# Hyperbolic attention of an adaLN-attention-FFN layer: projections and attention loop in one program, with loop steps between the last projections

## The chip, the cores and the metric

The kernel runs on one core of a Trainium2 chip. The metric is the device time of one execution in microseconds (us), the median of several runs. The engines of the core run beside each other and are ordered by semaphores alone: PE (matmuls), DVE (VectorE), ACT (ScalarE), POOL (GpSimd) and SP, which issues most of the DMAs.

## What is computed

The reference is one transformer layer on `x` of 32 x 64 x 256 in float32. Its stages are a mixture of eight experts and a shared one, a hyperbolic causal attention with a residual, three dense or routed feed-forward parts, a rotary attention and a last mixture of experts. The change lies in the hyperbolic attention:

```python
importance = sigmoid(x @ w_sur + b_sur)
spikes = importance > threshold
q, k, v = split(x @ W_qkv + b_qkv)           # 16 heads of 16
# for q and k, per head, with u0 the first element and u1.. the other fifteen:
nomin = sqrt(max(-u0**2 + sum(u1..**2), 1e-8))
time, space = cosh(nomin), sinh(nomin) * u1.. / nomin
neg_inner = tq @ tk.T - sq @ sk.T
scores = -arccosh(max(neg_inner, 1 + 1e-7))**2 / sqrt(16)     # causal
y = (softmax(scores) * spikes) @ v
x = x_residual + y @ W_out + b_out
```

## The kernel before

All of the stage's data stays in SBUF. There are 2048 tokens, in `NP = 16` blocks of 128 tokens and in `TT = 4` pieces of 512 (`TW`). Matrix products with W_qkv are made in three passes, because source and weights are split in a rounded part (`hi`) and a rest (`lo`).

`hyper_attention` has two programs, one after the other.

The first is the projection program. ACT rounds a piece of 512 tokens (`round_src`, L1703), DVE takes the rest (`split_src`, L1765). For each block i, PE makes q and k as one 512-column product in six matmuls, then v as 256 columns in six matmuls and one for the bias (L1682, L1688); both have two PSUM banks. DVE adds the bias and so takes q and k out of PSUM (L1852), ACT squares them (L1737) and takes v (L1742), and DVE sums the squares of each head (`space_norm`, L1784). v is copied by DMA to the places of both halves (L1663) and blocked out by head on ACT (`block_values`, L1711). The norms are a chain of 15 small DVE operations for half of the blocks at once (`norms`, L1796 to L1831), each waiting for the one before (`link`), and five exponentials on ACT (L1719 to L1725). Group 0 (blocks 0 to 7) runs between blocks 9 to 14, group 1 (blocks 8 to 15) behind the last block. The spike logits are 256 narrow matmuls of PE behind the last projection (L1694), then an exponential on ACT and three DVE operations (L1774 to L1778).

Then all engines meet at a barrier, and `hyper_units` begins. It is a software pipeline over 16 units of 128 query rows. Its loop has 25 steps; in step u each engine does the phases of the list `order`, phase with lag l for unit u - l. For one unit the path is: `stretch` on DVE scales q and k (L1538, lag 1), `turn` on PE transposes them (L1416, L1420, lag 1), `take_q` on ACT (L1493, 1), `block_k` on DVE (L1546, 2), `score` on PE (L1434, 3), `clamp` on DVE (L1553, 3), square, logarithm and root on ACT (L1498, L1502, L1506; 3, 4, 4), `root_add` on POOL (L1588, 4), logarithm and square on ACT (L1511, L1515; 4, 5), `mask` on POOL (L1593, 5), `top` on DVE (L1558, 6), `shift` on POOL (L1598, 5), `exponential` on ACT (L1522, 6), `p_turn` on PE and `p_take` on ACT (L1443, L1527; 7), `mix` on PE and `scale_y` on DVE (L1454, L1567; 8), and the output projection and the residual add (L1464 to L1576; 8, 9). Even units have 512 scores per row, odd ones 1024. Each engine executes its phases in the written order, so a phase that waits holds all that stand behind it on its engine.

Of the kernel before, what the change touches and what calls it, by code (L numbers as in the profile page):

```python
# [1250 lines left out]
class AttentionWeights:  # L1251


    def __init__(self, nc, m, ctx, raw, tag, w_qkv, w_out, b_qkv=None, b_out=None, w_sur=None, side=None):
# [7 lines left out]
        if b_qkv is not None:  # L1262
            self.bias, self.bo, self.ws = sb("bias", [P, 2 * D]), sb("bo", [P, KC]), sb("ws", [P, KC])
            self.vb = sb("vb", [P, D])
            self.loads += [(self.bo[:], col(b_out)), (self.ws[:], col(w_sur)),
                           (self.vb[:], b_qkv[2 * D:].unsqueeze(0).to_broadcast([P, D]))]
# [4 lines left out]
            self.vb_hi, self.vb_lo, self.vb_both, self.share = row("vb_hi", D), row("vb_lo", D), row("vb_both", D), row("share", P)  # L1271
        part = lambda name: sb(name, [P, KC, 3 * D], F32R)
        self.wq_hi, self.wq_lo = part("wq_hi"), part("wq_lo")

        self.wq = raw.enter_context(nc.sbuf_tensor(f"{tag}_wq", [P, KC, 3 * D], F32, side=side))
# [4 lines left out]
        self.loads.append((self.wq[:, :, QK:], rows(w_qkv)[:, :, QK:]))  # L1280
# [68 lines left out]
def hyper_units(nc, m, tag, resT, qk, v_blk, space, spike, wo, bo):  # L1349
# [6 lines left out]

    QK, GH, HP, VW, S = 2 * D, H // 4, H // 2, DH + 1, T // 2
    head4 = m.const[:, C_HEAD4:C_HEAD4 + GH]
    keys = (S, T)
    causal = [m.const[:, at:at + n].unsqueeze(1).to_broadcast([P, H, n]) for at, n in zip((C_FIRST, C_SECOND), keys)]  # L1360
    lag = dict(turn=1, q_blk=1, k_blk=2, score=3, clamp=3, root_sq=3, root_ln=4, root=4, root_add=4, dist_ln=4,
               dist=5, mask=5, top=6, shift=5, prob=6, p_turn=7, p_take=7, mix=8, y=8, y_turn=8, y_take=9, out=9,
               add=9, stretch=1)
    order = dict(tensor='out mix score p_turn y_turn turn',
                 scalar='root_ln dist root p_take prob q_blk root_sq dist_ln',
                 vector='y_take k_blk add top stretch y clamp', gpsimd='mask root_add shift')
    last = max(lag.values())
    sem = StageSemaphores(nc, tag)
    stretched, turned, k_turned, q_taken, k_blocked = (
        sem(n) for n in ("stretched", "turned", "k_turned", "q_taken", "k_blocked"))  # L1370
# [6 lines left out]
    with ExitStack() as s2:  # L1377
        sb2 = lambda name, shape: s2.enter_context(nc.sbuf_tensor(f"{tag}_{name}", shape, F32))
        x = sb2("x", [P, 2, QK])
        qT, k_blk = sb2("qT", [P, 4, KC, P]), sb2("k_blk", [P, 4, KC, 2, GH, T])  # L1380
        z, t, u = (sb2(n, [P, 2, H * T]) for n in ("z", "t", "u"))
        prob, pT = sb2("prob", [P, 2, H, T]), sb2("pT", [P, 2, HP, P])
        mx, rec = sb2("mx", [P, 2, H]), sb2("rec", [P, 2, H])
        y, yT = sb2("y", [P, 2, D]), sb2("yT", [P, 2, KC, P])
# [4 lines left out]
        yT_ps, o_ps = m.bank[7][:, 0:D], m.bank[7][:, D:2 * D]  # L1389
        by_head = lambda a, q: a[:, 0:H * keys[q]].rearrange("p (h t) -> p h t", t=keys[q])  # L1390
# [9 lines left out]
        def run(eng, name, phases):  # L1400

            for it in range(NP + last):
                for ph in order[name].split():
                    if 0 <= it - lag[ph] < NP:
                        phases[ph](it - lag[ph], (it - lag[ph]) % 2)

        with nc.Block() as block:
            @block.tensor
            def _(pe):
                def turn(i, q):  # L1410

                    pe.wait_ge(stretched, i + 1)
                    chunk = lambda n: x[:, q, n * P:(n + 1) * P]
# [24 lines left out]
                def p_turn(n, q):  # L1438

                    pe.wait_ge(prob_done, n + 1)  # L1440
                    wait(pe, p_taken, n)
                    for hp in range(HP):
# [4 lines left out]
                def mix(n, q):  # L1447

                    pe.wait_ge(p_taken, n + 1)
                    wait(pe, y_scaled, n)  # L1450
# [26 lines left out]

                issued = dict(y_turn=0, out=0)
                run(pe, "tensor", dict(turn=turn, score=score, p_turn=p_turn, mix=mix, y_turn=y_turn, out=out))

            def take_q(eng, copy, i, q):
                eng.wait_ge(turned, i + 1)
                wait(eng, scored, i // 2 * 2 - 2)
                copy(qT[:, i % 4].rearrange("p c n -> p (c n)"), qT_ps).then_inc(q_taken, 1)

            def take_y(eng, copy, n, q):
                eng.wait_ge(y_turned, n + 1)
                wait(eng, out_done, n - 1)
                copy(yT[:, q].rearrange("p c n -> p (c n)"), yT_ps).then_inc(y_taken, 1)
# [114 lines left out]


def hyper_attention(nc, m, tag, srcT, resT, w):

# [1896 lines left out]
```

## Time and profile before

| | us |
|---|---|
| median of 3 runs | 2069.12 (2066.55 to 2072.94) |
| the profiled execution, its time | 2071.58 |
| its span | 2069.8 |
| projection program, first source rounding to the last norm | 1114.2 to 1168.4 |
| loop program | 1169.2 to 1285.6 |

| engine | busy over the span | share |
|---|---|---|
| PE | 1923.5 | 93% |
| DVE | 1434.9 | 69% |
| ACT | 1105.4 | 53% |
| POOL | 849.8 | 41% |

All times inside the execution are counted from the start of the span. The busy shares are means over stages with different limits; the stage of the change takes 171 us of 2070, and only its own rows tell what it is worth.

### The profile page before, as it was taken

The page shows a single profiled execution, that of the slowest core. Times are in us where ns is not written, and L with a number is a line of the kernel's source. Part 1 is how long each engine was busy: PE and PEld are TensorE (multiplying, and loading weights), DVE is VectorE, ACT ScalarE, POOL GpSimd, SP SyncE. Part 2 cuts the span into 40 slices and gives each one's busy share as a digit, 9 for nine tenths or more (in the row PEclk, how much of TensorE's full clock was granted, in tenths as well). Part 3 has the DMA queues.
Part 4 walks back from the last instruction along what each step waited for, and adds up shares of the span by engine and source line. Part 5 has one row for each costly group of instructions (what it writes and reads, how often), then busy time and mean ns, then how long its engine had stood idle before and what let it go on. Part 6 is the DMA issues. An engine that isn't in the chain of part 4 may idle for free. (4 is left out here: it accounts for less than half of the span.)

```text
span 2069.8 us, 35351 instructions
## 1 busy us (share of the span) xinstructions
PE 1923.5 (93%) x12240; PEld 1620.3 (78%) x12240; DVE 1434.9 (69%) x2398; ACT 1105.4 (53%) x2118; POOL 849.8 (41%) x854
## 2 busy tenths in 40 slices
PE   8999999999999999999998677999999768959998
PEld 6788888888888888888887465788799646849998
DVE  7777676767767676776776896433589577857776
ACT  6555555545555554555544697232355365636664
POOL 7350321405032140504200185220399225968885
PEclk9999999999999999999999799999999779969999
DMA  4101010010101001010102201310156215556661
GB/s 155 62 1 62 1 61 0 20 41 0 61 0 61 0 23 37 0 61 0 29 1 62 62 3 42 123 41 11 63 192 211 65 26 148 185 204 209 213 214 45
DMA packets 96322, 144.51 MB, mean 70 GB/s; under 512 B 15358, under 2 KB 72608, under 8 KB 96096
## 3 DMA queue, kind: packets, MB, share of 16 engines
q1 hardware_dynamic: 89168, 127.21, 19.1%
q0 software_dynamic: 4928, 12.86, 1.8%
q10 hardware_dynamic: 2128, 3.15, 0.4%
q8 instruction: 60, 0.98, 0.2%
q14 instruction: 38, 0.31, 0.1%
HBM read 111.46 MB, written 14.16 MB: 61 GB/s over the span
## 5 line engine op out<-in xcount | busy, mean ns | idle before, releaser
L319 PE MATMUL ps<-cond_x_lo,cond_w_hi 128*128 128x512 f32 x1008 | 392.6, 389 | 0.0
L471 ACT ACTIVATE cond_h_hi<-cond_h 128x512 fp32r<-128x512 f32 x288 | 174.0, 630 | 289.7 <-DVE cond_h L666 289.6
L805 POOL TENSOR_TENSOR cond_w_lo<-cond_stage_up,cond_w_hi 128x512 fp32r<-128x512 f32 x36 | 47.1, 1308 | 591.8 <-ACT cond_w_hi L471 591.8
L319 PE MATMUL ps<-cond_x_hi_first,cond_w_hi 128*128 128x512 f32 x578 | 230.1, 398 | 3.1 <-DVE ps L652 2.5
L382 PE MATMUL ps<-cond_h_hi,cond_d_hi 128*128 128x512 f32 x576 | 224.8, 390 | 4.1 <-DVE cond_h_lo L671 4.1
L319 PE MATMUL ps<-cond_x_hi_first,cond_w_lo 128*128 128x512 f32 x578 | 225.2, 390 | 0.0
L382 PE MATMUL ps<-cond_h_hi,cond_d_lo 128*128 128x512 f32 x576 | 224.3, 389 | 0.0
L382 PE MATMUL ps<-cond_h_lo,cond_d_hi 128*128 128x512 f32 x576 | 224.2, 389 | 0.0
L319 PEld LDWEIGHTS ps<-cond_x_lo,cond_w_hi 128*128 128x128 f32 x1008 | 189.3, 188 | 37.2
L649 DVE TENSOR_TENSOR ps<-cond_p_row,ps 128x512 f32<-128x512 f32 x142 | 98.7, 695 | 170.7 <-PE ps L319 170.7
L524 ACT ACTIVATE cond_h<-ps 128x512 f32<-128x512 f32 x216 | 124.7, 596 | 164.8 <-DVE cond_h_lo L671 132.2
L671 DVE TENSOR_TENSOR cond_h_lo<-cond_h,cond_h_hi 128x512 fp32r<-128x512 f32 x288 | 199.5, 714 | 6.9
L471 ACT ACTIVATE cond_p_row<-ps 128x512 f32<-128x512 f32 x284 | 167.1, 597 | 39.8 <-PE ps L319 31.8
L666 DVE TENSOR_TENSOR cond_h<-cond_h,ps 128x512 f32<-128x512 f32 x216 | 147.6, 684 | 49.6 <-PE ps L319 49.6
L319 PE MATMUL ps<-cond_x_hi,cond_w_hi 128*128 128x512 f32 x430 | 167.6, 390 | 0.0
L319 PE MATMUL ps<-cond_x_hi,cond_w_lo 128*128 128x512 f32 x430 | 167.4, 389 | 0.0
L319 PEld LDWEIGHTS ps<-cond_x_hi_first,cond_w_hi 128*128 128x128 f32 x578 | 108.4, 188 | 39.1 <-DVE ps L652 12.1
L382 PEld LDWEIGHTS ps<-cond_h_hi,cond_d_hi 128*128 128x128 f32 x576 | 108.1, 188 | 28.3 <-issue 4.4
L659 DVE TENSOR_TENSOR cond_p_row<-cond_p_row,ps 128x512 f32<-128x512 f32 x142 | 97.3, 685 | 44.4 <-PE ps L319 44.3
L319 PEld LDWEIGHTS ps<-cond_x_hi_first,cond_w_lo 128*128 128x128 f32 x578 | 108.5, 188 | 22.9
L382 PEld LDWEIGHTS ps<-cond_h_hi,cond_d_lo 128*128 128x128 f32 x576 | 108.1, 188 | 22.9
L382 PEld LDWEIGHTS ps<-cond_h_lo,cond_d_hi 128*128 128x128 f32 x576 | 108.1, 188 | 22.6
(427 smaller groups left out, 5122.4 us busy)
## 6 DMA issues: line engine op xcount, KB each, us to landing
moe_stage_up<-in_L_ffn_expert_wv SPq DMA_DIRECT2D x22, 1024.0 KB, 7.9
typed_stage_up<-in_L_cond_wi SPq DMA_DIRECT2D x11, 1024.0 KB, 5.0
typed_stage_dn<-in_L_cond_wo SPq DMA_DIRECT2D x11, 1024.0 KB
moe_stage_dn<-in_L_ffn_expert_proj SPq DMA_DIRECT2D x11, 1024.0 KB
cond_stage_up<-in_L_cond_Wg SPq DMA_DIRECT2D x7, 1024.0 KB, 5.1
cond_stage_up<-in_L_cond_Wu SPq DMA_DIRECT2D x7, 1024.0 KB, 7.2
cond_stage_dn<-in_L_cond_Wd SPq DMA_DIRECT2D x7, 1024.0 KB, 9.5
rope_v_now<-rope_v_blk SPq DMA_DIRECT2D x16, 272.0 KB, 2.4
```

The lines of the kernel that those rows point to most:

```text
L319: ins = pe.matmul(bank, ws[:, j, u, w], xs.rearrange("p o n -> p (o n)"), start=(opens and k == 0), stop=(k == 2), skip_group_check=True)
L382: ins = pe.matmul(y_ps[side][d], w[:, 2 * j + r, d * P:(d + 1) * P], xs[:, tile], start=(j == 0 and r == 0 and k == 0), stop=(j == J - 1 a ...
L471: copy = lambda dst, src: act.activation(dst, src, ACT.Copy)
L524: act.activation(h[:, tile], src, ACT.Silu).then_inc(silu_done, 1)
L649: dve.tensor_tensor(bank_b[u], p1_row[:], bank_b[u], ALU.add).then_inc(u2_made, 1)
L659: dve.tensor_tensor(p5_row[:], p5_row[:], bank_b[u], ALU.add).then_inc(c22_made, 1)
L666: dve.tensor_tensor(h[:, tile], h[:, tile], src, ALU.mult).then_inc(h_made, 1)
L671: dve.tensor_tensor(h_lo[:, tile], h[:, tile], h_hi[:, tile], ALU.subtract).then_inc(h_ready, 1)
L805: return pool.tensor_tensor(w_lo[:, j, :, A11:A12 + 1], raw_up[:, :, :, upper(j)], w_hi[:, j, :, A11:A12 + 1], ALU.subtract)
```

## The change

The two programs become one, without a barrier in between.

- **Interleaving.** Step u of the loop stands behind the projection of block i = u + 11 (`DELAY`), so steps 0 to 4 stand between the last five projections, and steps 5 to 24 follow. The phases keep their lags and their order on each engine.
- **Norms.** Group 0 is blocks 0 to 6 (`FIRST = 7`), its four parts stand behind blocks 7 to 10. Group 1 is blocks 7 to 15: its first part stands ahead of step 5, two parts behind step 5 and the last behind step 6. The reciprocal and the division by it are gone: the first element of each head is written as half the cosh, and `stretch` multiplies only the other fifteen, in place in `qk`.
- **Stretch.** Blocks 0 to 6 are stretched by POOL, with lag 0; blocks 7 to 15 by DVE as before.
- **Exponentials and v.** The second five exponentials and the last three `block_values` stand behind steps 5, 6 and 7 on ACT.
- **Spikes.** `w_sur` stands twice beside W_qkv, and `b_sur` beside the bias, so that v's product has 258 columns and the 256 narrow matmuls are gone. ACT makes the exponential for each piece, DVE the comparison behind step 6, and eight small DMAs move the result to the rows of the units; `scale_y` of unit 0 waits for them.
- **First piece.** The first 512 tokens are rounded and split as 128 and 384.
- **Memory.** Projections use banks 4 to 7. Loop buffers lie over projection buffers; the reload of the residual is issued when the last v product is done, and a few waits guard these overlaps.

```diff
+    FIRST = 7
+    GROUPS, COUNTS = [slice(0, FIRST), slice(FIRST, NP)], [FIRST, NP - FIRST]
+    LINKS = 14
+    DELAY = FIRST + 4
+    AFTER = NP - DELAY
...
+        pieces = [(0, 0, P), (0, P, TW)] + [(tt, 0, TW) for tt in range(1, TT)]
+        late_steps = range(AFTER, NP + 10)
...
+            @block.sync
...
+                sp.wait_ge(v_done, NP)
+                sp.dma_start(resT[:].rearrange("p c n -> p (c n)"), m.x_saved).then_inc(m.x_back, 16)
+                sp.wait_ge(sp_steps, 3)
+                for q in range(2):
+                    for sq in range(4):
+                        row = sq % 2 * T + q * S
+                        sp.dma_start(spike[sq * S:(sq + 1) * S].rearrange("p (i q) -> p i q", q=2)[:, :, q],
+                                     sig[row:row + S].rearrange("p (i a) -> p i a", a=2)[:, :, sq // 2],
+                                     allow_slow_non_contiguous=True).then_inc(spike_moved, 16)
...
+            @block.tensor
+                def unit_steps(u):
+                    units(u, (out, 9), (mix, 8), (score, 3), (p_turn, 7), (y_turn, 8), (turn, 1))
...
+                for i in range(NP):
+                    project(i)
+                    unit_steps(i - DELAY)
+                for u in late_steps:
+                    unit_steps(u)
...
+            @block.scalar
+                def unit_steps(u):
+                    units(u, (root_log, 4), (dist, 5), (root_of, 4), (p_take, 7), (exponential, 6), (take_q, 1),
+                          (root_square, 3), (dist_log, 4))
...
+                    if i % SUB == SUB - 1:
+                        act.wait_ge(v_taken, i + 1)
+                        act.activation(sig[:, tt * SUB:(tt + 1) * SUB], v_row[:, tt % 2, :, D], ACT.Exp, scale=-1.0).then_inc(sp_small, 1)
...
+                    if i == FIRST + 1:
+                        exponentials(0)
+                    unit_steps(i - DELAY)
...
+                for u_step in late_steps:
+                    unit_steps(u_step)
+                    if u_step == AFTER:
+                        exponentials(1)
+                        block_values(TT - 2, 1)
+                    elif u_step == AFTER + 1:
+                        block_values(TT - 1, 0)
+                    elif u_step == AFTER + 2:
+                        block_values(TT - 1, 1)
...
+            @block.vector
+                def time_and_space(n, at, ser, cosh):
+                    table = m.const[:, C_SPACE:C_SPACE + 2 * H]
+                    dve.tensor_scalar(firsts(at), cosh, 0.5, None, ALU.mult).then_inc(spaced, 1)
+                    dve.tensor_tensor(space[:, at], ser, table.unsqueeze(1).to_broadcast([P, COUNTS[n], 2 * H]), ALU.mult)\
+                        .then_inc(spaced, 1)
...
+                def unit_steps(u):
+                    units(u, (take_y, 9), (block_k, 2), (add, 9), (top, 6), (stretch, 1), (scale_y, 8), (clamp, 3))
...
+                for i in range(NP):
+                    dve.wait_ge(qk_done, i + 1)
+                    dve.tensor_tensor(qk[:, i], qk_ps[i % 2], bias[:, 0:QK], ALU.add).then_inc(qk_taken, 1)
+                    if i >= 1:
+                        space_norm(i - 1)
+                    if FIRST <= i < FIRST + 4:
+                        norms(0, i - FIRST)
+                    if i % SUB == SUB - 1 and i // SUB + 2 < TT:
+                        split_src(i // SUB + 3, *pieces[i // SUB + 3])
+                    unit_steps(i - DELAY)
+                space_norm(NP - 1)
+                norms(1, 0)
+                for u_step in late_steps:
+                    unit_steps(u_step)
+                    if u_step == AFTER:
+                        norms(1, 1)
+                        norms(1, 2)
+                    elif u_step == AFTER + 1:
+                        norms(1, 3)
+                        spikes()
...
+            @block.gpsimd
+                def stretch(i, q):
+                    if i >= FIRST:
+                        return
+                    pool.wait_ge(spaced, 2)
+                    space_of = heads(qk[:, i])[:, :, 1:]
+                    pool.tensor_tensor(space_of, space_of, space[:, i].unsqueeze(2).to_broadcast([P, 2 * H, DH - 1]), ALU.mult)\
+                        .then_inc(stretched[0], 1)
...
+                def unit_steps(u):
+                    units(u, (stretch, 0), (mask, 5), (root_add, 4), (shift, 5))
```

## Rows read from the trace of the kernel before

**Rows 1.** Windows: length, busy us (count) of PE, PEld, DVE, ACT, POOL; granted clock; DMA.
```profile
1158.00:1169.20 11.20, 0.63 (x29) 0.54 (x29) 9.63 (x24) 6.59 (x12) 0.06 (x1) 0.55 0.22 47
1169.20:1189.00 19.80, 11.51 (x152) 6.59 (x152) 15.48 (x17) 10.61 (x17) 6.59 (x5) 0.59 0.01 2
...
1213.00:1225.00 12.00, 9.34 (x236) 7.13 (x236) 11.54 (x20) 11.85 (x18) 10.46 (x7) 1.00 0.01 3
```

**Rows 2.** Timeline, start of the projections: start us, us, engine line op.
```profile
1114.21 2.00 ACT L1703 ACTIVATE hyp_src_hi<-sum 128x1024 fp32r<-128x1024 f32 x2 [7.09 <-PEq L94]
1115.30 2.36 DVE L1765 TENSOR_TENSOR hyp_src_lo<-sum,hyp_src_hi 128x1024 fp32r<-128x1024 f32 x2 [2.12 <-ACT hyp_src_hi L1703]
1116.67 0.77 PE L1682 MATMUL ps<-hyp_wq_hi,hyp_src_hi 128*128 128x512 f32 x1 [5.02 <-DVE hyp_src_lo L1765]
```

**Rows 3.** Timeline of PE: block 11 begins, its v product begins, a warm turn.
```profile
1143.38 0.39 PE L1682 MATMUL ps<-hyp_wq_hi,hyp_src_hi 128*128 128x512 f32 x1
...
1144.78 0.28 PE L1682 MATMUL ps<-hyp_wq_hi,hyp_src_hi 128*128 128x256 f32 x1
...
1212.01 0.38 PE L1416 MATMUL ps<-const,hyp_x 128*128 128x128 f32 x2
```

**Rows 4.** Groups by shape, projection program: count, busy us, mean ns, idle before.
```profile
L1852 DVE TENSOR_TENSOR hyp_qk<-ps,hyp_bias 128x512 f32<-128x512 f32 x16 | 11.0, 689 | 8.0 <-PE ps L1682 7.9
L1784 DVE TENSOR_REDUCE hyp_r<-hyp_sq 128x32 f32<-128x480 f32 x16 | 10.3, 644 | 0.1
L1711 ACT ACTIVATE hyp_v_blk<-hyp_v_two,const 128x1024 f32<-128x1024 f32 x8 | 9.2, 1179 | 0.0
L1694 PE MATMUL ps<-hyp_ws,sum 128*32 128x1 f32 x256 | 3.1, 176 | 2.4 <-issue 2.4
```

**Rows 5.** Timeline of DVE, norms of group 1 and the spikes.
```profile
1158.86 0.62 DVE L1796 TENSOR_TENSOR hyp_sm<-hyp_qk 128x256 f32<-128x256 f32 x1
...
1160.95 0.43 DVE L1804 TENSOR_TENSOR hyp_ser<-hyp_ser,hyp_sm 128x256 f32<-128x256 f32 x1
...
1165.09 1.75 DVE L1824 RECIPROCAL hyp_below<-hyp_ser 128x256 f32<-128x256 f32 x1
...
1168.13 0.23 DVE L1778 TENSOR_SCALAR hyp_spike<-hyp_sig,threshold 128x16 f32<-128x16 f32 x1
```

**Rows 6.** Timeline of ACT: the five exponentials of group 0 and what follows.
```profile
1145.84 0.41 ACT L1719 ACTIVATE hyp_ln<-hyp_r 128x256 f32<-128x256 f32 x1
...
1147.57 0.63 ACT L1737 ACTIVATE hyp_sq<-hyp_qk 128x512 f32<-128x512 f32 x1
```

**Rows 7.** Timeline: turn of block 3 on PE, step 8 begins on ACT.
```profile
1179.08 0.63 PE L1420 MATMUL ps<-const,hyp_x 128*128 128x128 f32 x2
...
1199.37 0.71 ACT L1502 ACTIVATE hyp_t<-hyp_t,minus_one 128x512 f32<-128x512 f32 x1
```

**Rows 8.** Groups by shape, loop program: columns as in Rows 4.
```profile
L1546 DVE TENSOR_TENSOR hyp_k_blk<-ps,const 128x1024 f32<-128x1024 f32 x16 | 19.5, 1217 | 1.6 <-PE ps L1416 1.6
...
L1593 POOL TENSOR_TENSOR hyp_u<-const,hyp_t 128x512 f32<-128x512 f32 x8 | 8.9, 1107 | 3.4 <-ACT hyp_t L1515 3.4
```

**Rows 9.** Timeline of DVE and POOL: stretches beside POOL's operations.
```profile
1184.99 2.21 DVE L1538 TENSOR_TENSOR hyp_x<-hyp_qk,hyp_space 128x512 f32<-128x512 f32 x1
1216.35 0.68 DVE L1538 TENSOR_TENSOR hyp_x<-hyp_qk,hyp_space 128x512 f32<-128x512 f32 x1
1221.04 1.74 DVE L1538 TENSOR_TENSOR hyp_x<-hyp_qk,hyp_space 128x512 f32<-128x512 f32 x1
...
1219.84 2.39 POOL L1588 TENSOR_TENSOR hyp_z<-hyp_z,hyp_t 128x1024 f32<-128x1024 f32 x1
1222.20 1.49 POOL L1598 TENSOR_TENSOR hyp_u<-hyp_u,hyp_mx 128x512 f32<-128x512 f32 x1
```

**Rows 10.** DMA issues: size of one, median us from issue to landing.
```profile
hyp_bo<-in_L_attn_b_out SPq DMA_DIRECT2D x1, 1.0 KB, 2.5
...
xT<-x_saved SPq DMA_DIRECT2D x1, 2048.0 KB, 7.8
```

More of the change, by code:

```diff
@@ L1279, in __init__ @@
             self.loads += [(to[:, :, c, r], of[:, :, r, c]) for c, r in blocks]
-        self.loads.append((self.wq[:, :, QK:], rows(w_qkv)[:, :, QK:]))
+        self.loads.append((self.wq[:, :, QK:3 * D], rows(w_qkv)[:, :, QK:]))
+        if b_qkv is not None:
+            self.loads += [(self.wq[:, :, 3 * D + j], col(w_sur)) for j in range(2)]
         self.loaded, self.rounded, self.ready = (ctx.enter_context(nc.semaphore(f"{tag}_weights_{name}"))
@@ L1360, in hyper_units @@
     causal = [m.const[:, at:at + n].unsqueeze(1).to_broadcast([P, H, n]) for at, n in zip((C_FIRST, C_SECOND), keys)]
[L1361 to L1367, printed above, removed]
-    sem = StageSemaphores(nc, tag)
-    stretched, turned, k_turned, q_taken, k_blocked = (
-        sem(n) for n in ("stretched", "turned", "k_turned", "q_taken", "k_blocked"))
+    sem = StageSemaphores(nc, tag)
+    src_rounded, src_ready = sem("src_rounded"), sem("src_ready")
+    qk_done, v_done, qk_taken, v_taken = sem("qk_done"), sem("v_done"), sem("qk_taken"), sem("v_taken")
+    v_doubled, v_blocked, ones_set = [sem(f"v_doubled{i}") for i in range(2)], sem("v_blocked"), sem("ones_set")
+    sp_small, sp_steps, spike_moved = (sem(n) for n in ("spike_exp", "spike_steps", "spike_moved"))
+    squared, made, norm_act, norm, spaced = (sem(n) for n in ("squared", "made", "norm_act", "norm_steps", "spaced"))
+    bias_joined = sem("bias_joined")
+    stretched = [sem(f"stretched{i}") for i in range(2)]
+    turned, k_turned, q_taken, k_blocked = (sem(n) for n in ("turned", "k_turned", "q_taken", "k_blocked"))
     scored, clamped, root_squared, root_logged, rooted = (
@@ L1408, in _, with project @@
             @block.tensor
             def _(pe):
+                def project(i):
+                    q, at = i // SUB % 2, slice(i % SUB * P, (i % SUB + 1) * P)
+                    if i <= 1:
+                        pe.wait_ge(src_ready, i + 1)
+                    elif i % SUB == 0:
+                        pe.wait_ge(src_ready, i // SUB + 2)
+                    for ps, done, taken, cols in ((qk_ps, qk_done, qk_taken, slice(0, QK)),
+                                                  (v_ps, v_done, v_taken, slice(QK, 3 * D + 2))):
+                        if i >= 2:
+                            pe.wait_ge(taken, i - 1)
+                        n = 0
+                        more = cols.start == QK
+                        for k in range(KC):
+                            for x, wx in ((src_hi, wq_hi), (src_hi, wq_lo), (src_lo, wq_hi)):
+                                ins = pe.matmul(ps[i % 2], x[:, q, k, at], wx[:, k, cols], start=(n == 0),
+                                                stop=(n == 3 * KC - 1 and not more))
+                                n += 1
+                        if more:
+                            if i == 0:
+                                pe.wait_ge(bias_joined, 2)
+                            ins = pe.matmul(ps[i % 2], w.share[:], w.vb_both[:], start=False, stop=True)
+                        ins.then_inc(done, 1)
@@ L1495, in root_square, with take_q @@
+                def take_q(i, q):
+                    act.wait_ge(turned, i + 1)
+                    wait(act, scored, i // 2 * 2 - 2)
+                    act.activation(qT[:, i % 4].rearrange("p c n -> p (c n)"), qT_ps, ACT.Copy).then_inc(q_taken, 1)
                 def root_square(n, q):
@@ new lines, in spikes, with space_norm @@
+                def spikes():
+                    dve.wait_ge(sp_small, TT)
+                    dve.tensor_scalar(sig[:], sig[:], 1.0, None, ALU.add).then_inc(sp_steps, 1)
+                    dve.wait_ge(sp_steps, 1)
+                    dve.reciprocal(sig[:], sig[:]).then_inc(sp_steps, 1)
+                    dve.wait_ge(sp_steps, 2)
+                    dve.tensor_scalar(sig[:], sig[:], m.threshold[:], None, ALU.is_gt).then_inc(sp_steps, 1)
+                def space_norm(i):
+                    dve.wait_ge(squared, i + 1)
+                    dve.tensor_reduce(r2[:, i], heads(sq[:, i % 2])[:, :, 1:], AX_X, ALU.add).then_inc(made, 1)
```

459 lines of the change are left out of this document (188 added, 271 removed).

## The prediction

> **What bounds the kernel now.** I first read the windows. Over the whole span PE is busy 93%, but not here. From 1158.0 to 1169.2 PE works 0.63 us of 11.2 at a granted clock of 0.55, and DVE 9.63: the norms of group 1 are the wait that ends last. From 1169.2 to 1189 no engine is full, the loop is filling. From 1213 on ACT is busy 11.85 of 12 us and DVE 11.54 [rows 1]. So three regimes: DVE's chain at the seam, latency while the loop fills, ACT in the steady loop. What the change does to the steady loop is nothing; it can only move the time at which the loop is full. Then I took the timeline for the marks between which the sum is made: PE begins the projections at 1116.67 and block 11 at 1143.38 [rows 2, 3], ends the turn of block 3 (step 4) at 1179.08 + 0.63 = 1179.71, and ACT begins step 8 at 1199.37 [rows 7]. From there both kernels do the same work at the same pace, so the gain at ACT's step 8 is the gain at the end. Last I read the groups for prices.
>
> **Start of the projections.** Before, PE waits for a rounding and a subtraction of a whole piece, 1.0 and 1.2 us [rows 2]; both shrink to a quarter, and I keep 0.1 us each for what doesn't scale. Gain: 1.4 us. The rest of the piece is split long before block 1 needs it. The wider weights (1540 instead of 1536 elements) and the three more small loads lie under the expert stage and cost nothing; if that cover were gone, they are some 0.5 us each. v's 258 columns instead of 256 add under 1% of a 0.28 us matmul [rows 3].
>
> **From block 11 to the turn of block 3.** Before this takes 1179.71 - 1143.38 = 36.3 us.
> After, group 0 must be normed before POOL can stretch block 0. A block costs PE 2.2 us: 1144.78 - 1143.38 = 1.4 for q and k in six matmuls [rows 3], and seven of half the width for v, 7 x 0.12. DVE takes block 7 when its q and k are made, 4 x 2.2 - 1.5 = 7.3 us before 1143.38. From there it has: four takings with a sum of squares, 4 x 1.2 (0.69 and 0.64 long, starts a tenth closer [rows 4]); one source subtraction, 1.15; the parts of the norms at 7/8 of the old width. The old part 0 takes 1160.95 - 1158.86 = 2.1 us, the nine links to the reciprocal 4.1 [rows 5]; now 1.9, 3 x 1.25, and 0.65 for the two writes. Sum 4.8 + 1.15 + 1.9 + 3.75 + 0.65 = 12.3, so it ends about 5.0 us behind the old start of block 11. POOL's stretch has no row; its nearest is POOL's 512-element mask at 1.1 us, its dearest 512-element row 1.49 [rows 8, 9]. I take 1.25. The turn costs 0.6 warm [rows 3]. Block 0 is turned 5.0 + 1.25 + 0.6 = 6.8 us behind the mark; the projections 11 and 12 (2 x 2.2) lie under that.
> Then a ring closes for each of blocks 13 to 15: q and k product 1.4, taking and sum of squares 1.2, `block_k` 1.15 [rows 4, 8], turn 0.6, and 0.2 for two semaphores, together 4.55, since `block_k` is queued on DVE behind the taking of the next block and the turn on PE behind `block_k`. The v product lies under DVE's part. Three rings are 13.7 us; the first score adds 0.6. After: 6.8 + 13.7 + 0.6 = 21.1 us. Gain: 15.2.
> The old sequence in between is what vanishes: the reciprocal (1.75 us [rows 5]), the barrier, the tail of narrow matmuls [rows 4], and the norms of group 1, which are not gone but come later.
>
> **From the turn of block 3 to step 8 on ACT.** Before 1199.37 - 1179.71 = 19.7 us. Here the deferred work comes back. On DVE: one sum of squares 0.6; 14 links of 9/8 the width, 9/8 of the 6.2 us from 1158.86 to 1165.09, is 7.0; two writes 0.7; spikes 0.8 [rows 5]; together 9.1. Three stretches of blocks 4 to 6 leave DVE, 0.68 + 2.21 + 0.68 = 3.6 [rows 9]. Net 5.5. Behind part 2 of the norms, DVE waits for the five exponentials, which ACT does only behind its step 5: these are 1147.57 - 1145.84 = 1.7 us long [rows 6] and I count 1.6 of idle DVE. `block_k`, `top` and `clamp` of the next steps are queued behind that wait, and ACT and POOL wait for them. On ACT the last `block_values` (1.18 us [rows 4]) stands directly ahead of step 8: 1.1.
> Then the port. In the loop a stretch by DVE lasts 0.68 us when POOL rests and 1.74 when it starts inside POOL's 2.39 us `root_add`; it ends 0.55 us behind it, and POOL's next operation is drawn out to 1.49 [rows 9]. So an operation of DVE with two SBUF inputs waits for POOL's to end. Group 1 has eleven such links, and POOL has work in exactly these steps: stretches of blocks 5 and 6, `root_add` of units 1 and 2, a mask. I count four meetings: 1.0 with the stretch of block 5, and 1.1 + 2.0 + 1.0 (partly overlapped) with the stretch of block 6, the mask of unit 1 and `root_add` of unit 2, some 3.5 us in all with what DVE would have waited anyway taken off.
> Sum: 5.5 + 1.6 + 1.1 + 3.5 = 11.7. ACT's `block_values` and one of the meetings fall into the same wait once, so I take 1.1 back. Loss: 10.6.
>
> The Trainium skill ("SBUF — State Buffer", section "Who interferes with whom") says that DVE and GpSimd share a port pair as an exclusive lock, taken by DVE operations with two SBUF inputs and held for a whole instruction. The trace agrees with 0.68 against 1.74 us. The page counts `tensor_scalar` in a two-port mode among those that lock as well; with that the sum would gain nothing, at most a further meeting of about 1 us.
>
> **Spikes and residual.** The eight moves of 1 KB are issued behind the spikes, about 0.5 us each, and a DMA of 1 KB lands after 2.5 us [rows 10]: 6.5 us. From the spikes to the first `scale_y` DVE has more than that to do, so 0; they stand on SP behind the reload of the residual, which needs 7.8 us [rows 10] and is issued 20 us earlier. If the moves are late, DVE stands and `clamp` behind it: up to 3 us.
>
> **Sum.** 1.4 + 15.2 - 10.6 = 6.0 us. Made against the profiled span of 2069.8 (execution 2071.58, the wrapping of 1.8 us unchanged), it gives 2065.6 for such an execution, and off the median of 2069.12 it gives **2063.1**.
>
> **Rivals.**
> - *DVE's deferred chain finds the port free.* With no meetings, and the wait for the exponentials half filled, the loss is 5.5 to 7.5 instead of 10.6, and the gain 9 to 11: 2059. Its floor is ACT's own added work (1.7 and three `block_values`, 5.2 us): gain 11.4. For it: POOL is busy only 6.59 of 19.8 us in the filling loop [rows 1]. Against it: POOL is busiest in the very steps of the norms.
> - *The clock falls between the last projections; slower than before.* The ring of 4.55 us holds some 2.8 us of PE's work. The granted clock is 0.59 in a stretch where PE is busy 11.51 of 19.8 us, and 1.00 with 9.34 of 12 [rows 1]. At the lower level (1.2 GHz) a ring costs 1.4 more for q and k and 0.6 for the turn, the two blocks ahead of it 2 us each if they too are cold, and the scores 1: 3 x 2.0 + 4 + 1 = 11. It decides from the point at which also blocks 11 and 12 run low; then the gain of 6 turns to a loss of 5: 2074. If only the rings run low, 7 us go and it is 2070. The Trainium skill ("TensorE: Matmul & The Clock Gate", section "HAM oscillation — how this bites in real kernels") tells of kernels whose clock falls back in each gap between bursts; no row of this stage shows projections in bursts.
> - *The overlap does not come about.* If POOL's stretches take 3 us or more, the steps 0 to 4 slip behind the projections, and what is left is the start (1.4), the reciprocal's 1.75, the barrier's 0.8 and the narrow matmuls: 4 to 5 us, 2064.5. This is hard to tell from the forecast by the time alone.
>
> **How the numbers follow.** The forecast's own range is a gain of 3 to 9: 2060 to 2066; chance 0.52, of which a bit under half lies over 6.2 us. The free port 0.18, all over 6.2. The clock 0.20, half of it slower than 0.3%, the rest within. No overlap 0.10, within. About 0.3% (6.2 us) is what a measurement of this kernel can tell from no change. So faster 0.42, same 0.47, slower 0.11. The range for 8 in 10 runs from the free port, 2058, to the half-cold clock, 2071.
>
> **What would show it.** Right: PE begins the projections near 1115.3; the turn of block 3 ends near 1163; ACT begins step 8 near 1193; the period of two loop steps stays 11.8; links of group 1 in the timeline are 1 to 2 us long where a POOL operation runs beside them; the granted clock between blocks 11 and 15 is 0.9 or more. Wrong: matmuls of 0.6 us in blocks 12 to 15, a wait of DVE for the spike moves, a POOL stretch over 1.5 us, or a step 8 that begins before 1190.

## The result, and the profile after

The changed kernel takes 2076.72 us (median of 10 runs, 2074.03 to 2080.69), the kernel before 2068.34 beside it (10 runs): a ratio of 1.0038, 95% interval 1.0026 to 1.0050. It is slower; I had said 2063.1, and 2058 to 2071. Its profiled span is 2075.4 us, against 2069.8.

I lay the two timelines over each other from the last matmul of the expert stage, which lies ahead of everything the change is about. "Turn of block 3" is its end, "step 8" the start of `root_log` of unit 4.

| mark, us | before | after | predicted gain | gain |
|---|---|---|---|---|
| last matmul of the experts starts | 1111.27 | 1122.01 | 0 | **-10.7** |
| from it to the first projection | 5.40 | 4.30 | 1.4 | 1.1 |
| to the end of the turn of block 3 | 63.04 | 48.38 | 15.2 | 14.7 |
| to ACT's step 8 | 19.66 | 31.62 | -10.6 | -12.0 |
| ACT's step 8 to the last `root_log` (unit 15) | 64.63 | 64.20 | 0 | 0.4 |
| from there to the end of the span | 805.8 | 804.9 | 0 | 0.9 |

The stage itself gained 4.2 us. The experts, whose code is the same, lost 10.7. The marks of after, on PE (start of the projections, first product of block 11, turn of block 0, then the first product of blocks 13, 14 and 15, the turn of block 3) and on ACT (step 8), beside [rows 2, 3, 7]:

```profile
1126.31 0.77 PE L1474 MATMUL ps<-hyp_wq_hi,hyp_src_hi 128*128 128x512 f32 x1 [3.91 <-DVE hyp_src_lo L1687]
...
1153.77 0.50 PE L1474 MATMUL ps<-hyp_wq_hi,hyp_src_hi 128*128 128x512 f32 x1
...
1159.89 0.38 PE L1494 MATMUL ps<-const,hyp_qk 128*128 128x128 f32 x2
1160.03 0.48 PE L1474 MATMUL ps<-hyp_wq_hi,hyp_src_hi 128*128 128x512 f32 x1
...
1164.63 0.48 PE L1474 MATMUL ps<-hyp_wq_hi,hyp_src_hi 128*128 128x512 f32 x1
...
1169.86 0.48 PE L1474 MATMUL ps<-hyp_wq_hi,hyp_src_hi 128*128 128x512 f32 x1
...
1174.31 0.38 PE L1494 MATMUL ps<-const,hyp_qk 128*128 128x128 f32 x2
...
1206.31 0.70 ACT L1612 ACTIVATE hyp_t<-hyp_t,minus_one 128x512 f32<-128x512 f32 x1
```

The windows of after (length, then busy us of PE, PEld, DVE, ACT, POOL, the granted clock, DMA), beside [rows 1]: the clock is 1.00 (2.4 GHz) while the last projections and the first steps alternate, and falls when the projections are over and PE waits for DVE.

```profile
1144.00:1165.00 21.00, 18.45 (x108) 15.62 (x107) 17.66 (x34) 14.48 (x30) 4.87 (x5) 1.00 0.44 98
1165.00:1180.00 15.00, 7.28 (x98) 5.46 (x96) 11.33 (x15) 9.72 (x17) 3.23 (x4) 0.87 0.59 156
1180.00:1200.00 20.00, 7.31 (x110) 4.61 (x111) 15.96 (x22) 13.17 (x21) 9.87 (x7) 0.50 0.16 59
```

The deferred norms in after, on DVE. Unhindered, each of these links takes 0.46 us (the run without interleaving, below), L1744 0.41.

```profile
1176.60 1.18 DVE L1717 TENSOR_TENSOR hyp_r<-hyp_r,hyp_sm 128x288 f32<-128x288 f32 x1
...
1181.98 1.22 DVE L1724 TENSOR_TENSOR hyp_ser<-hyp_ser,hyp_sm 128x288 f32<-128x288 f32 x1
...
1186.11 0.46 DVE L1731 TENSOR_TENSOR hyp_sm<-hyp_ep,hyp_en 128x288 f32<-128x288 f32 x1 [1.93 <-ACT hyp_en L1598]
...
1190.93 1.14 DVE L1738 TENSOR_TENSOR hyp_ser<-hyp_ser,hyp_sm 128x288 f32<-128x288 f32 x1
1192.11 2.15 DVE L1739 TENSOR_TENSOR hyp_cosh<-hyp_ep,hyp_en 128x288 f32<-128x288 f32 x1
1194.30 1.38 DVE L1744 TENSOR_SCALAR hyp_qk<-hyp_cosh 128x288 f32<-128x288 f32 x1
```

What POOL does beside them. Its three operations end at 1191.76, 1193.93 and 1195.39; L1738, L1739 and L1744 of DVE end at 1192.07, 1194.26 and 1195.68, each 0.3 us behind one of them.

```profile
1190.49 1.27 POOL L1852 TENSOR_TENSOR hyp_qk<-hyp_qk,hyp_space 128x480 f32<-128x480 f32 x1
1191.72 2.21 POOL L1867 TENSOR_TENSOR hyp_u<-const,hyp_t 128x1024 f32<-128x1024 f32 x1
1193.90 1.49 POOL L1857 TENSOR_TENSOR hyp_z<-hyp_z,hyp_t 128x512 f32<-128x512 f32 x1
```

Who waits for it: `score` and `turn` on PE stand for `block_k`, which is queued behind the norms.

```profile
1180.17 1.11 PE L1508 MATMUL ps<-hyp_k_blk,hyp_qT 64*32 64x128 f32 x32 [5.47 <-DVE hyp_k_blk L1776]
...
1188.96 0.66 PE L1490 MATMUL ps<-const,hyp_qk 128*128 128x128 f32 x2 [4.75 <-DVE hyp_k_blk L1776]
...
1197.82 1.11 PE L1508 MATMUL ps<-hyp_k_blk,hyp_qT 64*32 64x128 f32 x32 [7.77 <-DVE hyp_k_blk L1776]
```

**The experts.** SP's issue of the gate weights tells the pace of the stage (start us, then the issue). In after, two issues that follow each other, one expert apart, and the last, six experts behind the first of them:

```profile
168.78 0.37 SPq L192 DMA_DIRECT2D cond_stage_up<-in_L_cond_Wg  x1
290.62 0.37 SPq L192 DMA_DIRECT2D cond_stage_up<-in_L_cond_Wg  x1
...
899.79 0.38 SPq L192 DMA_DIRECT2D cond_stage_up<-in_L_cond_Sg  x1
```

and in before:

```profile
168.52 0.37 SPq L192 DMA_DIRECT2D cond_stage_up<-in_L_cond_Wg  x1
289.12 0.37 SPq L192 DMA_DIRECT2D cond_stage_up<-in_L_cond_Wg  x1
...
891.94 0.38 SPq L192 DMA_DIRECT2D cond_stage_up<-in_L_cond_Sg  x1
```

Six experts take 731.0 us after and 723.4 before: 121.8 against 120.6 each. It is no wait and no clock: from 100 to 200 us PE is busy 100.00 us at a granted clock of 1.00 in both, with 438 matmuls before and 434 after. The matmuls themselves are longer. By operand, from the view of one line (count: shortest/median/longest ns, first and last start), after:

```profile
L319 PE MATMUL ps<-cond_x_hi_first,cond_w_hi x578: 387/396/506, 12.9 to 1112.2; 128*128 128x512 f32 x193
L319 PE MATMUL ps<-cond_x_hi,cond_w_hi x430: 389/393/504, 15.3 to 1114.9; 128*128 128x512 f32 x144
...
L382 PE MATMUL ps<-cond_h_hi,cond_d_hi x576: 387/397/500, 29.8 to 1121.6; 128*128 128x512 f32 x192
```

and before:

```profile
L319 PE MATMUL ps<-cond_x_hi_first,cond_w_hi x578: 389/389/507, 14.6 to 1101.4; 128*128 128x512 f32 x193
L319 PE MATMUL ps<-cond_x_hi,cond_w_hi x430: 387/389/481, 16.0 to 1104.2; 128*128 128x512 f32 x144
...
L382 PE MATMUL ps<-cond_h_hi,cond_d_hi x576: 387/389/501, 30.3 to 1110.8; 128*128 128x512 f32 x192
```

From start to start, by the unrounded times of the trace over these six experts (528 matmuls each), that is 230.8 ns on average instead of 228.3; leaving out the few steps over 300 ns, 230.8 instead of 227.4. The stage has the same code, but not the same addresses: v's bias rows are 8 bytes wider, the three weight buffers are 770 columns wide instead of 768, `ws` is gone, and every buffer is rounded up to 32 bytes. They lie ahead of the expert buffers, and push `x_hi`, `x_lo`, `w_hi`, `w_lo`, `d_hi`, `d_lo`, `h_hi` and `h_lo` back by 192 bytes per partition. `x_hi_first`, which lies over `xT`, and the staging buffers stay.

### The profile page after: what moved, and what is told of

It is laid out like the page before. It is cut to its first block and busy times, and to the rows that moved or that the text cites. A ratio compares the mean times of both kernels' runs of the same rounds, so it can differ in the third digit from the quotient of the medians.

```text
span 2075.4 us, 34832 instructions
## 1 busy us (share of the span) xinstructions
PE 1923.4 (93%) x11984; PEld 1614.1 (78%) x11984; DVE 1425.2 (69%) x2388; ACT 1105.2 (53%) x2122; POOL 854.3 (41%) x861
```

## The experiments: the addresses of the expert buffers

Theory A: the shift by 192 bytes costs the 10.7 us. The rival: something else of the new program does it (its code, its three more loads). "Per expert" is the distance of the first two issues above. First 64 bytes more in the changed kernel, so that the shift is 256:

```diff
+        sb("pad_x", [P, 16])
         xb = sb("x_hi", [P, 7 - IN_X, 2 * TW], F32R)
```

> The changed kernel with one unused 64-byte buffer ahead of the expert stage's buffers. In the changed kernel the wider weights push x_hi, x_lo, w_hi, w_lo, d_hi, d_lo, h_hi, h_lo of the expert stage by 192 bytes, so that they begin 64 bytes past a multiple of 128; with the pad they begin on multiples of 128 as in the kernel before. Theory A (the placement costs 1% of each expert matmul): the expert stage ends at 1111 us instead of 1122, and the whole is near 2064 us, 4 us under the kernel before. Rival B (the expert stage is slower for another reason, such as the program's code or the extra loads): the stage still ends at 1122 us and the whole stays near 2076.

Measured: 2066.35 us (10 runs; ratio to before 0.9989, interval 0.9976 to 1.0003), span 2065.4, 120.6 us per expert. The expert stage is back; the stage of the change takes 148.7 us from the last expert matmul to the last `root_log`, against 148.5 in after and 152.7 in before. With that, 4.0 us of the 6.0 that I had forecast are there, less than a measurement of this kernel can tell; the time itself, with an interval that holds 1, shows no gain over before.

The other way round, the kernel before with the same pad of 192 bytes (`[P, 48]`), with 64 (`[P, 16]`) and 128 (`[P, 32]`):

> The kernel before with an unused buffer of 192 bytes ahead of the expert stage's buffers and nothing else. Theory A: the expert stage gets the changed kernel's placement, one expert takes 121.8 us instead of 120.6, and the whole is 10 to 11 us slower than before, near 2079. Rival B: no difference.

> The kernel before with 64 bytes of pad. If what counts is the remainder by 128 bytes (theory A1), this is as slow as 192 bytes of pad, plus 10 to 11 us. If what counts is the distance moved, or the place relative to the buffers that don't move (theory A2), this differs from the 192-byte pad, by several us.

> The kernel before with 128 bytes of pad. A1: as before within 2 us, 2068. A2: another time than before. Rival B: as before too.

Measured: 2079.18 (5 runs, ratio 1.0056, 1.0036 to 1.0077), 2081.71 (5 runs, 1.0060, 1.0039 to 1.0081) and 2079.82 (10 runs, 1.0047, 1.0033 to 1.0062); 121.9, 121.8 and 121.7 us per expert. So the pad alone makes the kernel before as slow as the changed one: theory A holds, and nothing else of the change is needed. Alignment to 128 bytes is not it: the shift of 64 alone would have spoken for it, but a shift of 128, which keeps it, costs as much.

Then single groups of buffers. In the first, `pad` of `[P, 32]` stands ahead of `x_hi`, of `w_hi` and of `h_hi`; in the second ahead of `w_hi` and `h_hi`; in the third one of `[P, 64]` ahead of `x_hi`; in the fourth one of `[P, 32]` ahead of `xT`, and with it of everything.

> The kernel before, with only the streamed operands of the expert matmuls (x_hi, x_lo, h_hi, h_lo) moved by 128 bytes modulo 256; the loaded weights (w, d) are moved by 256. So far: moves of all buffers by 64, 128 and 192 bytes cost 1.1 to 1.3 us per expert (121.7 to 121.9 instead of 120.6), a move by 256 costs nothing. Theory C (the streamed operand must keep a place modulo 256): 121.7 us per expert. Theory D (the place of the loaded weights decides): 120.6. Theory E (the distance between streamed operand and weights decides): slow here and in the next one.

> The kernel before, with only the weights w and d moved by 128 bytes modulo 256, the streamed operands where they were (h by 256). Theory C: 120.6 us per expert. Theory D: 121.7. Theory E: slow, 121.7.

> The kernel before, all expert buffers moved by 256 bytes. If the placement repeats after 256 bytes, 120.6 us per expert as before. If the fast place was a chance of the exact addresses, anything up to 121.9.

> The kernel before with a pad of 128 bytes ahead of all SBUF buffers of the program, so that nothing moves against anything else, x_hi_first and the staging buffers included. If the absolute place modulo 256 counts: 121.7 us per expert. If only the distance between buffers counts (those moved in the former runs against x_hi_first, which stood still): 120.6.

Measured, one run each, before 2068.46 beside them: 2088.79, 2092.51, 2067.47 and 2070.44; 122.3, 122.7, 120.6 and 120.6 us per expert. The effect repeats at 256 bytes, and it does not hang on the address as such (the fourth) but on how the buffers lie to each other. The largest loss, 20 us up to the last expert matmul (1131.2, where before has 1111.3), comes where weights and streamed operands are 128 bytes apart in every matmul; there the whole distribution moves:

```profile
L384 PE MATMUL ps<-cond_h_lo,cond_d_hi x576: 390/393/404, 30.4 to 1131.0; 128*128 128x512 f32 x192
```

Two buffers had not been told apart from the rest: `x_hi_first`, and the staging buffers, which PE doesn't read.

```diff
+        sb("pad_all", [P, 32])
...
-        xa = nc.alloc_sbuf_tensor_at("cond_x_hi_first", [P, IN_X, 2 * TW], F32R, offset=m.xT_at)
+        xa = nc.alloc_sbuf_tensor_at("cond_x_hi_first", [P, IN_X, 2 * TW], F32R, offset=m.xT_at - 128)
```

> The kernel before, everything pushed 128 bytes as in the run of that name, but x_hi_first left where it was: so x_hi_first alone is 128 bytes away (modulo 256) from every other buffer, the staging buffers keep their distance to the weights. Theory E (the distance between what TensorE streams and the weights it loads costs): matmuls that stream x_hi_first, 0.38 of the up projection, become slower, h_hi and h_lo on d_hi and d_lo stay at 226.7 ns from start to start; 120.9 to 121.5 us per expert. Rival F (what costs is the distance between the staging buffers, which ScalarE, VectorE and GpSimd read and DMAs write, and the buffers of TensorE): 120.6 us per expert and a span of 2069.

```diff
-            room = aligned(nc.sbuf_base)
+            room = aligned(nc.sbuf_base) + 128
```

> The kernel before, only the staging buffers stage_up and stage_dn (and probs) moved by 128 bytes, all that TensorE reads unmoved. Theory E: 120.6 us per expert, span 2069. Rival F: 121.5 to 122 us per expert, span 2077 to 2082.

Measured, one run each, before 2068.22: 2075.86 and 2067.20; 121.6 and 120.7 us per expert. The issues, of `x_hi_first` moved alone:

```profile
168.64 0.37 SPq L192 DMA_DIRECT2D cond_stage_up<-in_L_cond_Wg  x1
290.21 0.37 SPq L192 DMA_DIRECT2D cond_stage_up<-in_L_cond_Wg  x1
```

and of the staging buffers moved alone:

```profile
167.72 0.37 SPq L192 DMA_DIRECT2D cond_stage_up<-in_L_cond_Wg  x1
288.39 0.37 SPq L192 DMA_DIRECT2D cond_stage_up<-in_L_cond_Wg  x1
```

Rival F is out: the place of the staging buffers, which other engines and DMAs use, does not count. (The other buffers of the stage that PE doesn't read, `h` among them, moved with `h_hi` in every run, so they are not told apart.) But my theory E is right in its sign only. It said that products of `h` and `d`, whose own distance is 0 in the first of these runs, would keep their pace. They did not: 232.2 ns on average from the start of `h_hi` on `d_hi` to that of `h_lo` on `d_hi` (63 pairs between 500 and 620 us, unrounded times), where before has 226.5. In before the median step is 226 or 227 ns for every kind of neighbours; in the slow placements the step from `h_hi` on `d_hi` to `h_lo` on `d_hi` is 230.6 to 232.7 on average. The start of the buffer in bytes, modulo 256 (only distances that are multiples of 64 were tried):

| kernel | x_hi_first | x_hi, x_lo | w, d | h | staging | us per expert |
|---|---|---|---|---|---|---|
| before | 128 | 128 | 128 | 128 | 64 | 120.6 |
| after, and before + 192 | 128 | 64 | 64 | 64 | 64 | 121.8, 121.9 |
| after + 64, before + 256 | 128 | 128 | 128 | 128 | 64 | 120.6 |
| before + 64 | 128 | 192 | 192 | 192 | 64 | 121.8 |
| before + 128 | 128 | 0 | 0 | 0 | 64 | 121.7 |
| x and h by 128 | 128 | 0 | 128 | 0 | 64 | 122.3 |
| w and d by 128 | 128 | 128 | 0 | 128 | 64 | 122.7 |
| everything by 128 | 0 | 0 | 0 | 0 | 192 | 120.6 |
| all but x_hi_first by 128 | 128 | 0 | 0 | 0 | 192 | 121.6 |
| staging by 128 | 128 | 128 | 128 | 128 | 192 | 120.7 |

All rows in which the buffers that PE reads agree are fast, all others slow. The mechanism behind it is open.

If the rule is one of the chip and not of this stage, it must show elsewhere. In the dense stage of before, `c_x_hi` and `c_x_lo` start at 160 (modulo 256), the weights and `h` at 32, and its matmuls start 230.6 ns apart (without steps over 300 ns).

```diff
+        sb("pad_w", [P, 32])
         w_hi = sb("w_hi", [P, ups, KC, F], F32R)
```

> The kernel before with only the 128 bytes ahead of the dense stage's w_hi. If the distance modulo 256 costs there as in the expert stage, 768 matmuls times 3.8 ns less: the stage from its first to its last up projection 176.1 to 173 us, span 2066.5 to 2067; without that effect 2069.

Measured: 2065.72 us (one run; before 2070.19), span 2063.9. From the first to the last up projection it is 172.8 us instead of 176.1; 3.3 us of 2.9 expected:

```profile
L1043 PE MATMUL ps<-c_x_hi,dense_w_hi x128: 389/389/792, 1296.0 to 1468.8; 128*128 128x512 f32 x128
```

The same products in before read 392/395/793, from 1296.5 to 1472.6; the step from start to start falls from 230.6 to 226.8 ns. It is more than one run: the stage takes 172.8 to 172.9 us in the three kernels of this study that have this pad, and 175.6 to 176.2 in all fourteen others. The rule holds in a second stage, for a distance of 128.

## The experiments: the stage of the change

All of these stand on the changed kernel with 64 bytes of pad. In the table, A is from the last expert matmul to the first projection, B to the end of the turn of block 3, C to the start of the last `root_log`.

| kernel | A | B | C | sum | time |
|---|---|---|---|---|---|
| before | 5.4 | 63.0 | 84.3 | 152.7 | 2068 to 2070 |
| padded after | 4.3 | 48.5 | 95.9 | 148.7 | 2066.35 |
| nine links left out | 4.3 | 50.2 | 90.5 | 144.9 | 2062.18 |
| reordered | 4.3 | 47.5 | 93.7 | 145.4 | 2058.79 |
| reordered, `ser` in PSUM | 4.3 | 47.5 | 90.6 | 142.4 | 2056.59 |
| no interleaving | 4.3 | 56.4 | 84.6 | 145.3 | 2059.60 |

B also holds what the clock did. The granted clock is 0.5 (1.2 GHz) in the first 5.0 us of B in before and 5.8 in padded after, but only in some 3 in the last three rows of the table; in the kernels that are before but for a pad, B is 61.9 us where this stretch lasts 3.3 and 63.4 where it lasts 5.8. And with nine links left out, a change that lies behind B, the clock also fell between the last projections, and B is 1.7 us longer than in padded after. These windows, of that kernel and then of padded after, show it:

```profile
1158.00:1162.00 4.00, 4.00 (x30) 3.28 (x15) 0.95 (x2) 0.90 (x2) 0.00 (x0) 0.57 0.00 0
```

```profile
1158.00:1162.00 4.00, 3.95 (x57) 2.91 (x49) 2.58 (x4) 2.03 (x6) 0.00 (x0) 1.00 0.01 4
```

The sum is 151.6 to 153.1 in all kernels whose stage is that of before. The rest of the span behind these marks differs by up to 8.5 us between profiled executions of the same code (800.1 and 808.6). So C is the column to read, and single times only beside it.

**What the deferred chain costs.**

```diff
-                    if u_step == AFTER:
-                        norms(1, 1)
-                        norms(1, 2)
-                    elif u_step == AFTER + 1:
-                        norms(1, 3)
+                    if u_step == AFTER + 1:
+                        time_and_space(1, GROUPS[1], r2[:, GROUPS[1]], r2[:, GROUPS[1]])
                         spikes()
```

> The padded kernel after, without nine links of group 1's norms (parts 1 to 3 but the last two writes; q and k of blocks 7 to 15 then get a wrong length). Base: the padded kernel, turn of block 3 ends 1163.3, ACT begins step 8 at 1194.9, 31.6 us. The nine links are 4.2 us unhindered, DVE's wait for the exponentials 1.9, the three meetings with GpSimd among them 3.1: 9.2. If DVE's chain is what fills the stretch, step 8 comes 6 to 9 us earlier (23 to 26 us behind the turn) and the span is 2056 to 2060. If ACT's added work (exponentials 1.7, three block_values 3.5) or the cold loop sets the end, it comes 0 to 3 us earlier.

Measured: step 8 begins 26.2 us behind the turn instead of 31.6, 5.4 earlier; C falls by 5.4. That is just below what I expected if DVE's chain fills the stretch, and above the rival's 0 to 3. The low clock is not what fills the stretch: after spent nearly all of it at a granted clock of 0.5, padded after had 1.00 from 1172 to 1175, and both take 31.6 us from the turn to step 8. The 9.2 us of DVE are worth 5.4, because DVE then waits for others, first for POOL's mask:

```profile
1181.05 1.22 DVE L1790 TENSOR_REDUCE hyp_mx<-hyp_u 128x16 f32<-128x1024 f32 x1 [2.65 <-POOL hyp_u L1865]
```

**The wait for the exponentials.** This kernel also has the pad of the dense stage.

```diff
                     if u_step == AFTER:
                         norms(1, 1)
-                        norms(1, 2)
+                        spikes()
                     elif u_step == AFTER + 1:
+                        norms(1, 2)
+                    elif u_step == AFTER + 2:
                         norms(1, 3)
-                        spikes()
```

> The padded kernel after with two edits in separate stages. First, on VectorE the spikes go behind part 1 of group 1's norms and parts 2 and 3 one step later each, so that the exponentials are made when it asks: the wait of 1.93 us goes; step 8 of ACT 1 to 2.5 us earlier relative to the end of the expert stage if the wait is on the path, 0 or later if the chain then meets GpSimd more often. Second, 128 bytes ahead of the dense stage's w_hi, so that weights, x and h of that stage are congruent modulo 256: now 230.5 ns from matmul to matmul there, against 226.7 in the expert stage; 768 matmuls times 3.8 ns is 2.9 us if placement is all. Together 3 to 5 us faster than the padded kernel (2066.35): 2061 to 2063; if the placement of the dense stage doesn't matter and the chain only moves, 2066.

Measured: 2058.79 us (4 runs, ratio 0.9953, 0.9937 to 0.9970). Step 8 begins 27.1 us behind the turn instead of 31.6, more than the 1 to 2.5 that I had expected, but of these 4.5 us only 2.2 are left at the last `root_log` (C). The wait of 1.93 is gone. The dense stage gives 3.3 (172.9 us instead of 176.2). The two make 5.5 us; the time is 7.6 below padded after (2061 to 2063 were expected), more than they explain. The chain, spread over three steps, meets POOL seven times and not five, and later steps pay:

```profile
1169.39 1.22 DVE L1726 TENSOR_TENSOR hyp_ser<-hyp_ser,hyp_sm 128x288 f32<-128x288 f32 x1
...
1176.78 2.15 DVE L1735 SCALAR_TENSOR_TENSOR hyp_ser<-hyp_ser,hyp_sm 128x288 f32<-128x288 f32 x1
...
1182.10 1.51 DVE L1739 SCALAR_TENSOR_TENSOR hyp_ser<-hyp_r,hyp_ser 128x288 f32<-128x288 f32 x1
1183.64 1.24 DVE L1740 TENSOR_TENSOR hyp_ser<-hyp_ser,hyp_sm 128x288 f32<-128x288 f32 x1
1184.92 2.52 DVE L1741 TENSOR_TENSOR hyp_cosh<-hyp_ep,hyp_en 128x288 f32<-128x288 f32 x1
```

**The port.** If the links are long because both operands come from SBUF while POOL works, one operand in PSUM must free them.

```diff
+                    if n == 1:
+                        ser = m.bank[7][:, 0:COUNTS[1] * 2 * H].rearrange("p (i g) -> p i g", g=2 * H)
+                        if part == 0:
+                            dve.wait_ge(v_taken, NP)
```

> The reordered kernel (2058.8), but ser of group 1 lies in PSUM (bank 7, free between v's last product and the first turn of y) instead of SBUF, so that seven of the fourteen links and the last write have at most one operand with an address in SBUF on their input side. There the links at 1169.39, 1176.78, 1182.10 and 1183.64 last 1.22, 2.15, 1.51 and 1.24 us beside GpSimd, 0.46 unhindered: 4.3 us. If the wait for the port is what draws them out, they last 0.5 us each, the turn of block 3 to the last root_log (93.7 us there) falls by 1 to 3 us (the rest of the 4.3 is met again by the next link that has two SBUF operands, or by the stretches), and the time is 2056 to 2058. If the length has another reason (their own latency behind the semaphore), they stay as long, and so does the time, 2058.8.

Measured: 2056.59 us (5 runs, before 2070.19; ratio 0.9939, 0.9926 to 0.9953), C lower by 3.0. The links with `ser`, on DVE, and POOL's `root_add` (1167.80) and `shift` (1179.58):

```profile
1169.41 0.46 DVE L1726 TENSOR_TENSOR ps<-ps,hyp_sm 128x288 f32<-128x288 f32 x1
...
1176.06 0.47 DVE L1735 SCALAR_TENSOR_TENSOR ps<-ps,hyp_sm 128x288 f32<-128x288 f32 x1
...
1180.86 0.45 DVE L1739 SCALAR_TENSOR_TENSOR ps<-hyp_r,ps 128x288 f32<-128x288 f32 x1
1181.34 0.47 DVE L1740 TENSOR_TENSOR ps<-ps,hyp_sm 128x288 f32<-128x288 f32 x1
```

```profile
1167.80 2.35 POOL L1864 TENSOR_TENSOR hyp_z<-hyp_z,hyp_t 128x1024 f32<-128x1024 f32 x1
...
1179.58 1.90 POOL L1879 TENSOR_TENSOR hyp_u<-hyp_u,hyp_mx 128x1024 f32<-128x1024 f32 x1
```

L1726 and L1739 lie wholly within POOL's operations and take 0.46 and 0.45 us. In the reordered kernel L1726, started at 1169.39 within this `root_add`, took 1.22:

```profile
1167.94 2.35 POOL L1860 TENSOR_TENSOR hyp_z<-hyp_z,hyp_t 128x1024 f32<-128x1024 f32 x1
```

So the operands in SBUF, and not the link's own latency, drew it out. This kernel has the lowest median of the study; against the reordered one the two intervals overlap, and the 3.0 us of C are the evidence.

**What the interleaving is worth.** `DELAY = NP` instead of `FIRST + 4`: one program, but every loop step behind block 15.

> The padded kernel after with DELAY = 16: one program, but no loop step between the projections; all loop steps follow block 15. It shows what the interleaving alone brings. Padded after: ACT's last root_log at 1259.2, 148.7 us behind the last matmul of the experts (1110.5); before: 152.7. My prediction's price for this case (start, reciprocal, barrier, narrow matmuls gone, loop from cold, but DVE's group 1 chain within the first steps) is 4 to 5 us better than before: 148 to 149, span 2065; if the chain of group 1 in the first steps takes the place of the old one, no better than before: 152 to 154, span 2069 to 2071.

Measured: 2059.60 us (one run), the last `root_log` 145.3 us behind the experts. I had expected 148 to 149, or 152 to 154; it is better than both, and 3.4 us better than the interleaved kernel on which it stands (the time is a single run). The chain of group 1 runs in one piece, with POOL at rest and the exponentials ready when it asks:

```profile
1154.86 0.66 DVE L1717 TENSOR_TENSOR hyp_sm<-hyp_qk 128x288 f32<-128x288 f32 x1
1155.55 0.46 DVE L1718 TENSOR_TENSOR hyp_r<-hyp_r,hyp_sm 128x288 f32<-128x288 f32 x1
...
1161.02 0.46 DVE L1740 TENSOR_TENSOR hyp_cosh<-hyp_ep,hyp_en 128x288 f32<-128x288 f32 x1
```

Fourteen links in 6.6 us. B is 7.9 us longer than in the interleaved kernel, but C is 84.6, as in before: 11.3 shorter. So the interleaving, as it was written, took 7.9 us out ahead of the mark and paid 11.3 behind it. Part of the difference is the clock at the start of B: against the two interleaved kernels whose low stretch was as short (47.5) it took out 8.9, and the net loss is 2.4 us instead of 3.4.

## Why the prediction was wrong, point by point

- **The step that failed** is the sentence that the wider weights lie under the expert stage and cost nothing. I had priced them as loads and as columns of a matmul, never as bytes that stand ahead of other buffers. They cost 10.7 us, through the addresses of a stage in whose code nothing changed. No case of mine held this; with the shift brought to 256 bytes (64 more) the kernel takes 2066.35, inside the range, and above the forecast's own 2060 to 2066 by a little. Its marks are near those I had named: the projections begin at 1114.8 (1115.3), the turn of block 3 ends at 1163.3 (1163), step 8 begins at 1194.9 (1193).
- **Start of the projections**: 1.1 instead of 1.4. Counted from the last expert matmul, DVE's first subtraction starts 0.63 us earlier than before (3.40 and 4.03), and it is itself 0.47 shorter; more of both stays than the 0.1 us each that I kept.
- **Block 11 to the turn of block 3**: from the start of block 11 it is 20.9 us, where I had 21.1, a gain of 15.4 instead of 15.2. The table's 14.7 also holds blocks 0 to 10, which took 27.5 us instead of 26.7; I had put that at nothing, and its cause was not looked for. The rings are 4.60 and 5.23 us, where I had 4.55; the second holds the first `score`. POOL's stretch takes 1.0 us and not 1.25.
- **Turn to step 8**: 12.0 instead of 10.6. The mis-sized term is the port: five meetings, and not four, with 0.72, 0.76, 0.68, 1.69 and 0.97 us beyond the unhindered length, 4.8 instead of 3.5. The fifth is L1744, a `tensor_scalar` with one input: 1.38 us against 0.41. The Trainium skill ("SBUF — State Buffer", section "Who interferes with whom") counts it among those that can take both ports; I had left that meeting out of the sum, and it was there. The wait for the exponentials was 1.93 instead of 1.6.
- **The steady loop** does not change: two steps take 11.73 us, 11.78 in before. **The spikes**: no wait of DVE for their moves.
- **The rivals.** The free port did not come about by itself, but its price was right: with the wait and `ser`'s meetings taken away C is 6.3 us longer than before, where I had said 5.5 to 7.5. The clock did not fall between the projections of after: 1.00 from 1144 to 1165, and still from 1172 to 1175. It did in one run of the same code up to there (nine links left out), for 3.4 us, with B 1.7 us longer; so the rival can happen, and was smaller there than the 7 to 11 us that I gave it. "The overlap does not come about" I had priced at a gain of 4 to 5 us; the run without interleaving gained 7.4 (6.3 to 6.6 against the variants of before whose clock was low as briefly at the start). So my comparison of the two cases had the wrong sign. I had set the whole gain ahead of the mark against the old kernel; 6.6 of its 14.7 us come without any interleaving (the reciprocal, the barrier, the narrow matmuls and group 0's earlier norms are in it; no run tells them apart), and the other 7.9, or 8.9 at the same clock, are fewer than the 11.3 by which C is longer when the chain runs among the loop steps.

## What to carry to other kernels

A buffer that grows moves all that is allocated behind it: after any change of a size, compare the matmul durations of stages that were not touched, and let the buffers that TensorE streams and loads start at the same place modulo 256 bytes, as in the fast rows of the table. Price an overlap against the nearest version without it, not only against the old kernel. A chain of small VectorE operations that is moved beside GpSimd's work should have one operand in PSUM, or stay where GpSimd rests.

## What the runs showed of the hardware

- The pace of a 128x512 float32 matmul depends on how the buffers lie to each other modulo 256 bytes: in the experts 227 ns from start to start where all agree, 230 to 233 where they don't (without steps over 300 ns), in the dense stage 226.8 and 230.6; 10.7 us of this kernel in the experts (20 in the worst placement), 3.3 in the dense stage. It concerns matmuls whose own operands agree as well (226.5 to 232.2 ns); moving the staging buffers, which TensorE doesn't read, changed nothing (120.7 us per expert). The Trainium skill ("SBUF — State Buffer", section "Who interferes with whom") lists TensorE's read ports for the streamed operand and the weights as independent; that alone gives no reason for such a difference, and the measurement decides.
- An operation of VectorE with one operand in PSUM ran within GpSimd's 2.35 us `root_add` at its full pace, 0.46 us; with both in SBUF it took 1.22 at the same place.
